# Attention outputs kept transposed: raw rows and softmax sums stored, scaled block by block on GpSimd, loaded as the projection's operand

## The chip, the cores and the metric

One core of a Trainium2 chip runs the whole program. The metric is the device time in microseconds (us) of that core, as a median of several runs. The engines named are TensorE (PE), VectorE (DVE), ScalarE (ACT), GpSimd (POOL) and SyncE (SP), which here only issues transfers.

## The reference

The program computes one transformer layer on 8 x 256 tokens of width 512: cross attention with 32 query heads in 8 key/value groups, then a mixture of experts. What the change touches is the end of the attention:

```python
score = jnp.einsum('bhqd,bhkd->bhqk', qh, kh) / math.sqrt(HEAD_DIM)
attn = jax.nn.softmax(score, axis=-1)
out = jnp.einsum('bhqk,bhkd->bhqd', attn, vh)
out = out.transpose(0, 2, 1, 3).reshape(N, S_, EMBED)
return out @ Wfc.T + bfc
```

Before it the input is normalised and q, k, v are projected. After it come the residual, a second normalisation, a router over 8 experts, a shared expert of double width, and two routed experts for each token.

## The kernel before, in words

Engines run queues of their own, in an order written out by hand, and meet at semaphores. Nothing reorders: an instruction that waits holds up everything behind it on its engine.

**Attention** runs over 16 units: unit u is block u // 4 (512 tokens, 2 of the 8 sequences) and head quarter u % 4 (8 heads). A unit has four groups j of 4 heads and one sequence; G = 4u + j counts them to 64. For each G, PE makes four score fills (line 1303), ACT four exponentials (line 1027), and PE multiplies the probabilities by V in two parts (`pv_part`, line 1317). V carries a column of ones, so that each head's output of 16 rows comes with a 17th, the softmax sum, in strips of 32 partitions of one PSUM bank. Between them PE fills scores for the row maxima of unit u + 2 (line 1231), which DVE reduces (line 1699, four for a pair of groups); at j = 0 PE transposes the maxima of unit u + 1 and DVE negates them (`neg_max_part`, lines 1756 and 1759). After each G, ACT copies the 256 columns of output out of PSUM (`attn_out`, line 1018). After each pair of groups PE transposes the outputs (`pair_transpose`, line 1334), DVE takes the reciprocals of the sums (line 1826) and multiplies (line 1828), and SP stores a unit's rows to `attn_dram` (line 516).

**GpSimd beside it** runs a loop t = 0 to 15. For t < 10 it waits for the maxima of unit t + 2 or so (`nm_done`), cuts half an expert's weights into two 16-bit parts (`cut_weights`: lines 820, 803, 813) and issues the load of the half after next (line 791). For all t it loads a tile of x (line 835), adds the output bias (line 840) and stores the sum as `xb_dram` (line 842). After the loop it loads and cuts the ten held weight halves h (`load_held`, line 794; lines 803 and 813 for even h, while DVE takes odd h at line 1928), and then the shared expert's down weights (lines 860, 864).

**Projection stage**, 16 tiles t of 128 tokens: SP loads a tile's attention rows (line 532) and its `xb` row (line 535). PE transposes the attention rows (line 1395), ACT copies them (line 1037), PE projects (`out_project`, line 1403), DVE adds the residual (`residual_norm`, line 1892) and normalises (line 1902), PE transposes again (line 1412) and computes the router's logits (line 1421). ACT also makes the first part of held half h = t - 2 within tile t (`first_part`, line 1069). SP and ACT both wait for all 16 `xb` stores ahead of the stage. The experts follow (lines 1467 and 1479).

## Time and profile before

| | |
|---|---|
| median of 3 runs | 791.48 us (788.52 to 794.94) |
| the profiled execution's own time | 791.93 us |
| its span | 790.1 us |
| attention, from first to last score and V product | about 103 to 294 us |
| projection stage, to the first product of the experts | about 296 to 383 us |
| experts | about 383 to 790 us |

The span is the time from the program's first to its last instruction in the profile; about 1.8 us lie around it. All times of rows are counted from the span's start.

### The profile page before, as it was taken

Reading aid. Unit: us, or ns where it says so; the run is one execution under the profiler, and the core shown is the slowest. Engines: PE = TensorE matmul, PEld = TensorE weight load, DVE = VectorE, ACT = ScalarE, POOL = GpSimd, SP = SyncE. Lnnn points to the kernel's source line nnn. Section 1 sums busy time; section 2 is a strip of 40 time slices with the busy share of each in tenths; the row PEclk is TensorE's granted clock in tenths of the full one; section 3 lists DMA queues with packets and bytes.
Section 4 is the critical chain, followed back from the end, with each engine's and each line's share of the span. In section 5 each row is a group of like instructions: output and inputs, shape, how many; then the busy total and the mean of one; then the engine's idle time right before and its main releaser. Section 6 shows DMA issues by size and latency. Waiting matters only on the chain.

```text
span 790.1 us, 16078 instructions
## 1 busy us (share of the span) xinstructions
PE 760.1 (96%) x5151; PEld 407.0 (52%) x5152; DVE 579.7 (73%) x1194; ACT 429.3 (54%) x843; POOL 269.3 (34%) x224
## 2 busy tenths in 40 slices
PE   6998999999999989999999999999999999999897
PEld 4553533343433325656755556555555555555553
DVE  4777779999999976998789886555555555547666
ACT  3666579999999973566433553434344343322231
POOL 3263008999993301665300101111111111015331
PEclk9999989999999999999999999999999999999999
DMA  8898846556645798998598576876777777559985
GB/s 330 324 405 245 250 139 211 185 168 194 195 121 172 228 331 295 331 376 275 173 232 225 137 173 137 187 174 175 183 175 180 179 180 173 126 164 288 288 240 150
DMA packets 161782, 172.07 MB, mean 218 GB/s; under 512 B 103680, under 2 KB 117504, under 8 KB 161216
## 3 DMA queue, kind: packets, MB, share of 16 engines
q1 hardware_dynamic: 150012, 128.89, 56.5%
q0 software_dynamic: 11120, 41.43, 16.8%
q10 hardware_dynamic: 596, 1.07, 0.4%
q8 instruction: 30, 0.49, 0.3%
q14 instruction: 24, 0.20, 0.1%
HBM read 105.40 MB, written 42.73 MB: 187 GB/s over the span
## 4 chain that ended last, share of the span: by engine, by line
PE 77%; DVE 10%; DMA 7%; ACT 2%; issue 2%; SPq 1%; DVEq 0%; ACTq 0%
PE psum L1467 29%; PE psum L1479 15%; PE psum L1317 8%; PE psum L1303 6%; PE psum L1231 4%; PE psum L1403 4%; PE psum L1207 4%; PE psum L1334 2%; DMA sb_weights<-in_wdn 2%; DMA sb_weights<-attn_dram 2%; PE psum L1183 1%; DMA sb_hT<-sb_h 1%; DMA sb_weights<-x_dram 1%; DMA sb_weights<-in_ctxT 1%; DVE sb_rows L1902 1%
## 5 line engine op out<-in xcount | busy, mean ns | idle before, releaser
L1467 PE MATMUL psum<-sb_weights,sb_rows 128*128 (+1 forms) x1608 | 250.8, 313 | 0.5 <-DMA sb_rows<-xnT_dram 0.5
L1467 PEld LDWEIGHTS psum<-sb_weights,sb_rows 128*128 128x128 f16 x1608 | 157.2, 98 | 91.8 <-DMA sb_rows<-xnT_dram 1.0
L1027 ACT ACTIVATE sb_weights<-psum,sb_rows 128x512 f32<-128x512 f32 x256 | 158.3, 683 | 16.9 <-PE psum L1303 15.0
L1699 DVE TENSOR_REDUCE sb_rows<-psum 128x4 f32<-128x1024 f32 x128 | 149.9, 1213 | 5.5 <-PE psum L1231 5.5
L1479 PE MATMUL psum<-sb_weights,sb_hT 128*128 (+1 forms) x630 | 147.4, 379 | 2.2 <-DMA sb_hT<-sb_h 2.2
L894 POOL DMA_INDIRECT sb_rows<-xn_rows,sb_slot_tok x39 | 38.2, 980 | 218.1 <-DVE sb_rows L2288 147.9
L1479 PEld LDWEIGHTS psum<-sb_weights,sb_hT 128*128 128x128 f16 x630 | 61.4, 98 | 67.5 <-DMA sb_hT<-sb_h 3.1
L1303 PE MATMUL psum<-sb_weights 50*128 50x512 f16 x256 | 90.0, 391 | 3.0 <-ACT sb_weights L1027 2.6
L1096 ACT ACTIVATE psum<-psum 128x352 f32<-128x352 f32 x71 | 31.8, 448 | 111.8 <-DVE psum L1949 111.8
L1317 PE MATMUL psum<-sb_weights 128*32 128x256 f32 x1024 | 82.9, 396 | 0.0
L1231 PE MATMUL psum<-sb_weights 48*128 48x256 f16 x512 | 73.2, 275 | 0.5 <-DVE sb_rows L1699 0.4
L914 POOL DMA_INDIRECT sb_weights<-slot_y,sb_p_i x32 | 31.4, 982 | 82.7 <-DMA slot_y<-sb_rows 41.7
L1949 DVE SCALAR_TENSOR_TENSOR psum<-psum,sb_inv_now,sb_h 128x352 f32<-128x352 f32 x39 | 23.1, 593 | 49.2 <-PE psum L1467 49.2
L1403 PE MATMUL psum<-sb_weights 128*128 128x512 f32 x128 | 58.5, 600 | 0.0
L1303 PEld LDWEIGHTS psum<-sb_weights 50*128 50x128 f16 x256 | 23.5, 93 | 63.5 <-ACT sb_weights L1027 59.3
L1962 DVE SCALAR_TENSOR_TENSOR sb_h<-psum,sb_h_scale_i,sb_h 128x352 f16<-128x352 f32 x71 | 41.3, 582 | 18.8 <-ACT sb_h L1101 18.6
L1091 ACT ACTIVATE sb_h<-psum,sb_inv_now 128x352 f32<-128x352 f32 x39 | 21.6, 553 | 55.2 <-PE psum L1467 55.2
L1101 ACT ACTIVATE sb_h<-psum,sb_h_scale_i 128x352 f16<-128x352 f32 x71 | 39.3, 553 | 17.2 <-DVE sb_h_scale_i L1954 17.2
L1207 PE MATMUL psum<-sb_weights 128*128 128x512 f16 x192 | 44.9, 380 | 3.7 <-issue 1.9
L803 POOL TENSOR_TENSOR sb_weights<-sb_weights,sb_w_scale_i 128x1408 f32<-128x1408 f32 x15 | 38.5, 2570 | 28.0 <-ACT sb_weights L1069 27.2
L1091 ACT ACTIVATE sb_h<-psum,sb_w_inv_i 128x352 f32<-128x352 f32 x32 | 17.7, 554 | 55.0 <-PE psum L1467 39.2
L813 POOL TENSOR_TENSOR sb_weights<-sb_weights 128x1408 f16<-128x1408 f32 x15 | 42.9, 2861 | 1.2
(264 smaller groups left out, 1017.9 us busy)
## 6 DMA issues: line engine op xcount, KB each, us to landing
sb_weights<-in_wgu SPq DMA_DIRECT2D x20, 704.0 KB, 7.4
sb_weights<-in_wgu POOLq DMA_DIRECT2D x20, 704.0 KB, 5.6
sb_weights<-in_wdn SPq DMA_DIRECT2D x17, 768.0 KB, 5.9
slot_y<-sb_rows SPq DMA_DIRECT2D x39, 256.0 KB, 2.3
sb_weights<-q_parts SPq DMA_DIRECT2D x96, 64.0 KB, 2.2
x_dram<-sb_rows SPq DMA_DIRECT2D x24, 256.0 KB, 4.6
q_parts<-sb_weights SPq DMA_DIRECT2D x16, 256.0 KB, 4.6
sb_rows<-in_x POOLq DMA_DIRECT2D x16, 256.0 KB, 4.8
```

The lines of the kernel that those rows point to most:

```text
L813: nc.gpsimd.tensor_tensor(low, stage, high, ALU.subtract).then_inc(gu_cut, 1)
L1027: nc.scalar.activation(probs[G % 2][:, kt, pair * 512:(pair + 1) * 512], bank[4 + f % 2], ACT.Exp, scale=exp_scale[:, n:n + 1]).then_inc(e ...
L1091: nc.scalar.activation(silu_out[par], two_parts(bank[GU_BANKS[par][0]]), ACT.Silu, scale=inv).then_inc(sil_done, 1)
L1207: mm = nc.tensor.matmul(bank[Q_BANKS[n][m]], wq16[:, wp, k, m * P:(m + 1) * P], xnT[n % 2][:, xp, k, :], start=(k == 0 and i == 0), stop=( ...
L1231: mm = nc.tensor.matmul(bank[banks[qt] + side][:, h * SEQ:(h + 1) * SEQ], q_st[s][lo:hi, g, h, b * SEQ + qt * P:b * SEQ + (qt + 1) * P], k ...
L1303: nc.tensor.matmul(bank[4 + side].rearrange("p (h t) -> p h t", h=HH), k_st[s][lo:hi, g, b * SEQ + kt * P:b * SEQ + (kt + 1) * P], q_st[s] ...
L1317: mm = nc.tensor.matmul(bank[6][VW * c:VW * (c + 1), 0:SEQ], v_now, probs[G % 2][:, kt, c * SEQ:(c + 1) * SEQ], start=(kt == 0), stop=(kt ...
L1403: mm = nc.tensor.matmul(bank[2 + s][:], oT[s][:, k, :], wfc_sb[:, k, :], start=(k == 0), stop=(k == KD - 1))
L1467: mm = nc.tensor.matmul(bank[GU_BANKS[par][which]][:, 0:F], x_T[:, xp * D + k * P:xp * D + (k + 1) * P], gu(wp, k, which), start=(k == 0 a ...
L1479: mm = nc.tensor.matmul(bank[Y_BANKS[par]][:], hT[par][:, hp, j, :], dn(wp, j), start=(j == 0 and n == 0), stop=(j == NF - 1 and n == 2))
L1699: nc.vector.tensor_reduce(to[:, :, j // UB, :, j % UB, qt], psum[:, banks[qt] * 512:(banks[qt] + 2) * 512] .rearrange("p (a h k) -> p a h ...
L1962: nc.vector.scalar_tensor_tensor(h16[par][:, 1, 0:F], bank[GU_BANKS[par][1]][:, 0:F], h_scale[:, par:par + 1], h16[par][:, 0, 0:F], ALU.mu ...
```

## The change

ACT no longer copies after each group but 512 columns after each pair of groups. SP stores a unit's raw transposed rows (`o_parts`, four transfers) and its sums (`o_sums`, one). PE's `pair_transpose` and DVE's normalisation disappear. For each block of four units, GpSimd loads the sums, DVE takes 128 x 128 reciprocals in one instruction (`sum_recs`) at a fixed place in its order (j = 3 of units 5, 9 and 13, and tile 2 of the projection stage for the last block), and GpSimd stores them (`o_recs`). GpSimd then handles each of the 16 units as a chunk i: two loads (rows, and reciprocals repeated over 16 partitions), a multiplication of 128x512, and a store in 512-byte pieces to `attnT_dram`. Chunks 0 to 10 lie in iterations t = 5 to 15 of its loop, chunk 11 behind the loop, chunks 12 to 15 among the held halves. The projection loads its operand in that layout, up to four tiles ahead; the transposes of line 1395 and ACT's copies of line 1037 are gone.

```diff
-    attn_dram = dram("attn_dram", (TILES, P, D))
+    o_parts = dram("o_parts", (BLOCKS, KD, P, BT))
+    o_sums = dram("o_sums", (BLOCKS, KD, MG * HPG, BT))
+    o_recs = dram("o_recs", (BLOCKS, KD, MG * HPG, BT))
+    attnT_dram = dram("attnT_dram", (TILES, P, KD, P))
...
+        chunk_raw, chunk_rec = [words(at, D) for at in chunk_at], [words(at + D, D) for at in chunk_at]
+        def chunk_set(i):
+            return 0 if i < 6 else 1 if i < 3 * KD else 1 + i % 2
...
             def store_attn(u):
-                sp.wait_ge(attn_done, UG * (u + 1))
-                n, m = u // KD, u % KD
-                sp.dma_start(attn_dram[n * TPB:(n + 1) * TPB, :, m * P:(m + 1) * P].rearrange("a p c -> p a c"),
-                             attn_u[u % 2]).then_inc(attn_st[u % 2], 16)
+                sp.wait_ge(pv_evac, MG * (u + 1))
+                n, m, st = u // KD, u % KD, o_st[u % 2]
+                sp.dma_start(o_sums[n, m].rearrange("(g c) t -> c g t", c=HPG),
+                             st[HD:HD + VW * (HPG - 1) + 1:VW]).then_inc(attn_st[u % 2], 16)
+                for c in range(HPG):
+                    sp.dma_start(o_parts[n, m].rearrange("(g c d) t -> c d g t", g=MG, c=HPG)[c],
+                                 st[VW * c:VW * c + HD]).then_inc(attn_st[u % 2], 16)
...
-            def load_attn(b, s):
-                sp.dma_start(a_in[s], attn_dram[bass.ds(b * 2 + s, 1)].rearrange("o p d -> (o p) d")).then_inc(a_ld[s], 16)
+            def load_attn(t):
+                if t >= TPB:
+                    sp.wait_ge(fc_ready, t - TPB + 1)
+                sp.wait_ge(chunk_st, 16 * KD * (t // TPB + 1))
+                sp.dma_start(oT_rows[t % TPB], attnT_dram[t].rearrange("p k t -> p (k t)")).then_inc(a_ld[t % TPB], 16)
...
                 if u == 15:
-                    sp.wait_ge(attn_st[0], FREE + 16 * BATCH)
+                    sp.wait_ge(attn_st[0], FREE + O_ST * UNITS // 2)
                     for s in range(2):
                         sp.wait_ge(xb_st[s], 16 * TILES // 2)
-                    load_res_rows(0, 0)
+                    for s in range(2):
+                        load_res_rows(0, s)
                 store_attn(u)
                 if u == 13:
-                    for s in range(2):
-                        sp.wait_ge(attn_st[s], FREE + 16 * 2)
                     sp.wait_ge(gu_cut, CUTS_P2)
-                    for s in range(2):
-                        load_attn(0, s)
+                    for t in range(TPB):
+                        load_attn(t)
...
+            def load_sums(n):
+                for s in range(2):
+                    pool.wait_ge(attn_st[s], FREE + O_ST * KD // 2 * (n + 1))
+                nc.gpsimd.dma_start(sum_sb, o_sums[n].rearrange("m h (q t) -> (m h q) t", t=P)).then_inc(sum_ld, 16)
+            def store_recs(n):
+                pool.wait_ge(rec_done, n + 1)
+                nc.gpsimd.dma_start(o_recs[n].rearrange("m h (q t) -> (m h q) t", t=P), sum_sb).then_inc(rec_st, 16)
+            def load_chunk(i):
+                n, m, s = i // KD, i % KD, chunk_set(i)
+                pool.wait_ge(rec_st, 16 * (n + 1))
+                if i > 0:
+                    pool.wait_ge(chunk_st, 16 * (i - i % 2 if i >= (BLOCKS - 1) * KD else i))
+                nc.gpsimd.dma_start(chunk_raw[s], o_parts[n, m]).then_inc(chunk_ld, 16)
+                nc.gpsimd.dma_start(chunk_rec[s],
+                                    o_recs[n, m].unsqueeze(1).broadcast_to([MG * HPG, HD, BT])).then_inc(chunk_ld, 16)
+            def scale_chunk(i, loaded):
+                n, m, s = i // KD, i % KD, chunk_set(i)
+                pool.wait_ge(chunk_ld, 32 * loaded)
+                nc.gpsimd.tensor_tensor(chunk_raw[s], chunk_raw[s], chunk_rec[s], ALU.mult).then_inc(chunk_done, 1)
+                pool.wait_ge(chunk_done, CHUNK_SEEN + i + 1)
+                nc.gpsimd.dma_start(attnT_dram[n * TPB:(n + 1) * TPB, :, m, :].rearrange("a p t -> p a t"),
+                                    chunk_raw[s].rearrange("p (a t) -> p a t", a=TPB)).then_inc(chunk_st, 16)
             pool.wait_ge(w_fc, 48)
             load_x(0)
             for t in range(TILES):
                 if t < CUTS_P2:
                     pool.wait_ge(nm_done, t + 3)
+                i = t - TPB - 1
+                if i >= 0:
+                    load_chunk(i)
+                if t % TPB == 0 and t > 0:
+                    load_sums(t // TPB - 1)
+                if t < CUTS_P2:
                     cut_weights(t)
                 if t + 1 < TILES:
                     load_x(t + 1)
                 add_bias(t)
+                if i >= 0:
+                    scale_chunk(i, i + 1)
+                if t % TPB == 0 and t > 0:
+                    store_recs(t // TPB - 1)
+            load_chunk(3 * KD - 1)
+            scale_chunk(3 * KD - 1, 3 * KD)
...
-            pool.wait_ge(attn_done, UNITS * UG)
+            pool.wait_ge(pv_evac, UNITS * MG)
+            load_sums(BLOCKS - 1)
             pool.wait_ge(dn_max_done, NE + SH)
             for h in range(3):
                 load_held(h)
+            store_recs(BLOCKS - 1)
+            last = (BLOCKS - 1) * KD
             for c in range(CUTS_P2, CUTS):
                 h = c - CUTS_P2
+                if h == 0:
+                    for i in range(last, last + 2):
+                        load_chunk(i)
                 if h % 2 == 0:
                     scale_weights(c)
                     second_part(c)
                 else:
                     pool.wait_ge(gu_cut_v, h // 2 + 1)
+                if h == 1:
+                    for i in range(last, last + 2):
+                        scale_chunk(i, last + 2)
+                    for i in range(last + 2, last + 4):
+                        load_chunk(i)
+                if h == 3:
+                    for i in range(last + 2, last + 4):
+                        scale_chunk(i, last + 4)
...
-            def attn_out(G):
-                act.wait_ge(pv_ready, G + 1)
-                if G >= 4:
-                    act.wait_ge(ot_ready, G // 2 - 1)
-                nc.scalar.copy(o_raw[G % 4], bank[6][:, 0:SEQ]).then_inc(pv_evac, 1)
+            def attn_out(p):
+                u, g = p // MG, p % MG
+                act.wait_ge(pv_ready, UB * (p + 1))
+                act.wait_ge(attn_st[u % 2], FREE + O_ST * (u // 2))
+                nc.scalar.copy(o_st[u % 2][:, g, :], bank[6]).then_inc(pv_evac, 1)
...
-                if G > 0:
-                    attn_out(G - 1)
-            attn_out(UNITS * UG - 1)
-            def ot_evac(t, s):
-                act.wait_ge(ota_ready, t + 1)
-                nc.scalar.copy(oT[s], bank[s][:].rearrange("p (k t) -> p k t", k=KD)).then_inc(ota_evac, 1)
+                if G > 0 and G % UB == 0:
+                    attn_out(G // UB - 1)
+            attn_out(UNITS * MG - 1)
...
-                if kt == 0 and G > 0:
-                    pe.wait_ge(pv_evac, G)
+                if kt == 0 and G > 0 and b == 0:
+                    pe.wait_ge(pv_evac, G // UB)
                 v_now = v_res[u // KD][:, b * UB + kt, MG * (u % KD) + g, :]
                 for c in range(HPG):
-                    mm = nc.tensor.matmul(bank[6][VW * c:VW * (c + 1), 0:SEQ], v_now,
+                    mm = nc.tensor.matmul(bank[6][VW * c:VW * (c + 1), b * SEQ:(b + 1) * SEQ], v_now,
...
-            def ot_transpose(t, s, n):
-                pe.wait_ge(a_ld[s], n * 16 + 16)
-                if not (isinstance(t, int) and t < 2):
-                    pe.wait_ge(ota_evac, t - 1)
-                for k in range(KD):
-                    tr = nc.tensor.transpose(bank[s][:, k * P:(k + 1) * P], a_in[s][:, k * P:(k + 1) * P], ident[:])
-                tr.then_inc(ota_ready, 1)
-            def out_project(t, s):
-                pe.wait_ge(ota_evac, t + 1)
+            def out_project(t, r, n):
+                pe.wait_ge(a_ld[r], n * 16 + (16 + A_SEEN))
...
+            def sum_recs(n):
+                dve.wait_ge(sum_ld, 16 * (n + 1))
+                nc.vector.reciprocal(sum_sb, sum_sb).then_inc(rec_done, 1)
...
-                if j % 2 == 1 and G > 2:
-                    normalise(G - 3)
+                if j == UG - 1 and u % KD == 1 and u > 1:
+                    sum_recs(u // KD - 1)
...
+                if t == 2:
+                    sum_recs(BLOCKS - 1)
...```

DVE's order around unit 9, before (the two copies of the normalisation, lines 1826 and 1828, stand at j = 1 and j = 3):

```order
L1756 TENSOR_SCALAR sb_rows<-psum 32x128 [waits nm_in2,mxt_ready]
L1759 SCALAR_TENSOR_TENSOR sb_rows<-psum,sb_rows 32x128 [waits nm_first]
L1699 TENSOR_REDUCE sb_rows<-psum 128x2x2 [waits max_ready] x2
L1826 RECIPROCAL sb_rows<-psum 128x16 [waits ot_ready]
L1828 TENSOR_TENSOR sb_rows<-psum,sb_rows 128x4x64 [waits rec_done]
L1699 TENSOR_REDUCE sb_rows<-psum 128x2x2 [waits max_ready] x4
```

And in the changed kernel (`tile_cmp` holds the block's sums, `sum_ld` counts their loads by GpSimd):

```order
L1765 TENSOR_SCALAR sb_rows<-psum 32x128 [waits nm_in0,mxt_ready]
L1768 SCALAR_TENSOR_TENSOR sb_rows<-psum,sb_rows 32x128 [waits nm_first]
L1708 TENSOR_REDUCE sb_rows<-psum 128x2x2 [waits max_ready] x6
L1831 RECIPROCAL sb_tile_cmp<-sb_tile_cmp 128x128 [waits sum_ld]
L1708 TENSOR_REDUCE sb_rows<-psum 128x2x2 [waits max_ready] x2
```

The normalisation after every pair of groups is gone, and between the maxima of every fourth unit stands one instruction that waits for a transfer that GpSimd issues.

GpSimd's iteration t = 8, before:

```order
L820 TENSOR_TENSOR sb_weights<-sb_weights,sb_w_scale_i 128x1408 [waits gu_ld0,nm_done]
L803 TENSOR_TENSOR sb_weights<-sb_weights,sb_w_scale_i 128x1408 [waits gu_first]
L813 TENSOR_TENSOR sb_weights<-sb_weights 128x1408 [waits gu_scaled]
L835 DMA sb_rows<-in_x 128x512 [waits xb_st1,gu_cut]
L840 TENSOR_TENSOR sb_rows<-sb_rows,sb_weights 128x512 [waits xb_ld0]
L842 DMA xb_dram<-sb_rows 128x512 [waits xb_done]
```

And in the changed kernel:

```order
L853 DMA sb_weights<-o_parts 128x512 [waits chunk_st,rec_st,nm_done]
L854 DMA sb_weights<-o_recs 128x1x512
L842 DMA sb_tile_cmp<-o_sums 128x128 [waits attn_st1,attn_st0]
L815 TENSOR_TENSOR sb_weights<-sb_weights,sb_w_scale_i 128x1408 [waits gu_ld0]
L798 TENSOR_TENSOR sb_weights<-sb_weights,sb_w_scale_i 128x1408 [waits gu_first]
L808 TENSOR_TENSOR sb_weights<-sb_weights 128x1408 [waits gu_scaled]
L830 DMA sb_rows<-in_x 128x512 [waits xb_st1,gu_cut]
L835 TENSOR_TENSOR sb_rows<-sb_rows,sb_weights 128x512 [waits xb_ld0]
L837 DMA xb_dram<-sb_rows 128x512 [waits xb_done]
L860 TENSOR_TENSOR sb_weights<-sb_weights 128x512 [waits chunk_ld]
L862 DMA attnT_dram<-sb_weights 128x4x128 [waits wq_low]
L846 DMA o_recs<-sb_tile_cmp 128x128 [waits rec_done]
```

Chunk 3 and the sums of block 1 have come in: five transfers and a multiplication more, and at its top a wait for the store of the chunk before (`chunk_st`).

## Rows read from the trace of the kernel before

**Rows 1.** Two stretches: length; busy PE, PEld, DVE, ACT, POOL; clock; DMA share; GB/s.
```profile
180.00:210.00 30.00, 30.00 (x312) 11.87 (x316) 28.26 (x37) 27.78 (x52) 28.25 (x18) 1.00 0.59 188
330.00:360.00 30.00, 27.61 (x124) 16.74 (x123) 27.42 (x54) 16.81 (x33) 16.54 (x11) 1.00 1.01 374
```

**Rows 2.** Timeline of ACT, two pairs of groups (start, us, instruction, idle before).
```profile
205.59 2.43 ACT L1027 ACTIVATE sb_weights<-psum,sb_rows 128x512 f32<-128x512 f32 x4 [0.31 <-PE psum L1303]
207.93 0.37 ACT L1018 COPY sb_rows<-psum 128x256 f32<-128x256 f32 x1
208.22 2.49 ACT L1027 ACTIVATE sb_weights<-psum,sb_rows 128x512 f32<-128x512 f32 x4
210.60 0.37 ACT L1018 COPY sb_rows<-psum 128x256 f32<-128x256 f32 x1
211.44 2.43 ACT L1027 ACTIVATE sb_weights<-psum,sb_rows 128x512 f32<-128x512 f32 x4 [0.47 <-PE psum L1303]
```

**Rows 3.** Timeline of PE: the transposes of one pair.
```profile
204.58 0.66 PE L1334 MATMUL psum<-sb_ident,sb_rows 128*128 128x128 f32 x4
```

**Rows 4.** Timeline of GpSimd, from the start of t = 4 to that of t = 7.
```profile
168.68 2.54 POOL L820 TENSOR_TENSOR sb_weights<-sb_weights,sb_w_scale_i 128x1408 f16<-128x1408 f32 x1
...
200.45 0.58 POOL L791 DMA_DIRECT2D sb_weights<-in_wgu  x1 [0.30 <-POOL sb_weights L813]
...
201.58 1.29 POOL L840 TENSOR_TENSOR sb_rows<-sb_rows,sb_weights 128x512 f32<-128x512 f32 x1
203.16 0.56 POOL L842 DMA_DIRECT2D xb_dram<-sb_rows  x1 [0.30 <-POOL sb_rows L840]
203.75 2.55 POOL L820 TENSOR_TENSOR sb_weights<-sb_weights,sb_w_scale_i 128x1408 f16<-128x1408 f32 x1
```

**Rows 5.** GpSimd again: a load that waits for a store; the first held halves.
```profile
237.50 0.56 POOL L842 DMA_DIRECT2D xb_dram<-sb_rows  x1 [0.30 <-POOL sb_rows L840]
240.77 0.54 POOL L835 DMA_DIRECT2D sb_rows<-in_x  x1 [2.70 <-DMA xb_dram<-sb_rows]
...
298.79 1.60 POOL L794 DMA_DIRECT2D sb_weights<-in_wgu  x3 [31.46 <-DVE sb_dn_max L1836]
315.18 2.71 POOL L803 TENSOR_TENSOR sb_weights<-sb_weights,sb_w_scale_i 128x1408 f32<-128x1408 f32 x1 [14.79 <-ACT sb_weights L1069]
...
321.12 0.59 POOL L794 DMA_DIRECT2D sb_weights<-in_wgu  x1 [0.30 <-POOL sb_weights L813]
323.00 0.55 POOL L794 DMA_DIRECT2D sb_weights<-in_wgu  x1 [1.29 <-DVE sb_weights L1928]
...
342.99 0.58 POOL L794 DMA_DIRECT2D sb_weights<-in_wgu  x1 [0.30 <-POOL sb_weights L813]
```

**Rows 6.** DMA issues from 100 to 300 us: KB each, us to landing.
```profile
sb_weights<-q_parts SPq DMA_DIRECT2D x78, 64.0 KB, 2.2
sb_rows<-in_x POOLq DMA_DIRECT2D x16, 256.0 KB, 4.8
xb_dram<-sb_rows POOLq DMA_DIRECT2D x16, 256.0 KB, 3.7
```

**Rows 7.** GpSimd's indirect gathers (line 894): ns min/median/max, start.
```profile
L894 POOL DMA_INDIRECT sb_rows<-xn_rows,sb_slot_tok x39: 940/940/2364, 449.9 to 664.1; - x39
```

**Rows 8.** Timeline of DVE in unit 9, j = 3, and in tile 0.
```profile
222.82 0.26 DVE L1826 RECIPROCAL sb_rows<-psum 128x16 f32<-128x16 f32 x1 [0.18 <-PE psum L1334]
...
302.86 0.69 DVE L1892 TENSOR_TENSOR sb_rows<-psum,sb_rows 128x512 f32<-128x512 f32 x1 [4.66 <-PE psum L1403]
```

**Rows 9.** Groups of DVE by line, 100 to 400 us: busy, mean ns.
```profile
L1826 DVE RECIPROCAL sb_rows<-psum 128x16 f32<-128x16 f32 x32 | 7.9, 247 | 2.9 <-PE psum L1334 2.7
L1656 DVE RECIPROCAL sb_rs_a<-sb_std 128x1 f32<-128x1 f32 x16 | 2.5, 154 | 0.5 <-ACT sb_std L1051 0.5
```

**Rows 10.** Timeline of SP: the first load of an `xb` row.
```profile
294.63 0.33 SPq L535 DMA_DIRECT2D sb_rows<-xb_dram  x1
```

**Rows 11.** Landing of GpSimd's weight loads (line 794), min/median/max.
```profile
DMA to landing us min/median/max: 5.5/7.0/9.8
```

136 lines of the change are left out of this document (44 added, 92 removed).

## The prediction

> **What bounds the kernel now.** I read the busy times by stretch first. In the middle of the attention PE is busy all of 30 us, DVE 28.3, ACT 27.8 and GpSimd 28.3 [rows 1]: four engines are within 8% of full, so taking work from one gains little, and giving work to any costs at once. Then the timeline of ACT: two groups take 211.44 - 205.59 = 5.85 us, with idle times of 0.31 and 0.47 us that end with PE's scores [rows 2]; those come behind the pair's transposes, 0.66 us on PE [rows 3]. So ACT and PE set the pace together, a unit in 11.7 us. Then GpSimd: iterations t = 4 to 6 take (203.75 - 168.68) / 3 = 11.69 us, with no idle time beyond 0.3 us behind its own instructions [rows 4]. GpSimd is already as slow as a unit. In the projection stage (330 to 360 us) DVE is busy 27.4 of 30 us, and the DMA engines all the time [rows 1].
>
> **The change, part by part.** The sum is made against the profiled execution's 791.9 us, 0.4 above the median.
>
> *PE, ACT and DVE in the attention.* The transposes go. Two copies of 0.37 us, each of which holds up the next exponential by 0.29 (207.93 to 208.22) [rows 2], become one of 512 columns, which I put at their sum of 0.58. ACT can give back at most its idle times, 0.3 to 0.5 us of 5.85. I take 5.55 us a pair, 11.1 a unit: 32 x 0.3 = 9.6 us, if nothing else waits. PE's next limit is then ACT itself. DVE loses about 0.7 us a pair. SP issues five stores a unit where it issued one, about 2 us more at 0.4 each in 11.1 us; it stays ahead.
>
> *GpSimd's iterations.* A chunk adds two load issues of 0.56, a multiplication of 128x512 (1.28, as the bias of the same size), 0.3 until it is seen, and a store issue of 0.56 [rows 4]: 1.1 + 2.2 us. At the top it waits for the store before. The row for that wait: a store issued at 237.50 lets the next load start at 240.77, 3.3 us later [rows 5], so 2.7 behind its issue. Iterations 6 and 7 thus take 11.7 + 1.1 + 2.2 + 2.7 = 17.7 us, against a unit's 11.1. For 64 KB of sums or reciprocals I take 2.6 us to landing (2.2 for 64 KB on SP, 3.7 for GpSimd's stores of 256 KB [rows 6]).
>
> Step by step, from the span's start: t = 4 begins at 168.7 as before [rows 4], and adds two issues: t = 5 begins at 181.5. It waits 2.0 for the reciprocals' store: 17.0 us, to 198.5. Iterations 6 and 7: to 233.9. In t = 8 the load of block 1's sums is issued behind chunk 3's loads, at 233.9 + 2.7 + 1.1 = **237.7**, and lands at 240.3.
>
> *DVE's wait.* The instruction that needs it stands where DVE is at 222.82 before (unit 9, j = 3) [rows 8]; at the new pace that is 103 + 119.8 x 5.55 / 5.85 = 216.7. DVE stands still from 216.7 to 240.3. Behind it are the maxima of unit 11; PE gets through about one more group of scores, then ACT starves too. The reciprocals take 1.0 us by the slope between 1 and 16 elements, (247 - 154) / 15 = 6.2 ns each [rows 9], so DVE goes on at 241.3, **18.5 us later than before** at this place. The 9.6 us saved are no part of the sum from here on: GpSimd sets the time.
>
> *The second such wait.* GpSimd: rest of t = 8 (0.6 + 11.1 + 2.2 + 0.6) to 252.2; t = 9, 2.0 + 1.1 + 11.1 + 2.2, to 268.6. From t = 10 no cut hides the loads: 2.7 + 0.6 + 4.8 to landing [rows 6] + 2.2 = 10.3 us each, to 289.2. In t = 12 the sums' load is issued at 293.0, and DVE is released at 296.6. DVE gets there four units after 241.3, at 285.7, and before at 222.8 + 46.8 = 269.6: now 27.0 later. The attention's rest of 24.7 us ends at about 320, not 294.3.
>
> *The start of the projection stage.* SP and ACT want all 16 `xb` stores. The last is issued in t = 15: 289.2 + 10.9 (t = 12) + 9.6 (t = 13) + 10.3 (t = 14) = 320.0, and 5.4 into t = 15, at 325.4. It lands at 329 (3.7 [rows 6]). SP's first `xb` row was asked for at 294.63 [rows 10]; now at 329, landed at 334. DVE's first tile starts at 334, not 302.9 [rows 8]: **+31 us**.
>
> *The held halves.* GpSimd ends t = 15 at 330.3 and chunk 11 at 340.6, and issues the first held load at 341.2 (298.8 before [rows 5]); with 7.0 to landing [rows 11] tile 2 barely waits. Block 3's reciprocals come after tile 2: 315.5 + 31 + 1.0 = 347.6, stored and landed at 350.2. Four chunk loads, 2.2, to 352.4. Half 0 (5.9, as 315.18 to 321.12) to 358.3; before 321.1 [rows 5]: +37. In h = 1: 0.6 + two scalings and stores 4.4 + wait 2.7 + four issues 2.2, so half 4 is asked for at 368.2, before 323.0: +45. h = 2 to 374.7, h = 3 with chunks 14 and 15 to 379.7, h = 4 to 386.2, before 343.0: +43. ACT's first parts sit inside the tiles' order, so the tiles follow these loads. Two or three us come back as later loads are prefetched, and from tile 12 on each tile may gain up to 0.6 (the transposes of line 1395 gone): +40 at the stage's end. The experts are unchanged. The down weights' cuts end about as much later as the stage does, and keep their lead.
>
> **Sum:** 791.9 + 40 = **832 us**.
>
> *Rule against row.* The store row gives 3.3 us until a dependent load can start. The Trainium skill (DMA: Bandwidth & Descriptors, "Anatomy of one DMA") gives a GpSimd transfer about 2.0 us plus its bytes over 436 GB/s, an estimate of 2.6 us for 256 KB. By the rule each of some ten such waits would be 0.7 shorter, and the time about 826 by estimate; the rows go first.
>
> **Bounds.** All new transfers at the fastest rows: stores 2.6 between issue and dependent start, loads 3.0, sums 2.2, weights 5.5 [rows 11]. Some ten waits are then 0.7 shorter, eight loads 1.8, and three weight loads 1.5: about 26 us less in all, 806. Dearer: the trace has no plain GpSimd store in 512-byte pieces and no repeated load. The nearest from above are the indirect gathers at 0.94 us [rows 7]; at 0.38 more for each of some 60 new issues on the path, 22 us, 854; with landings a little slower, 858. I take 0.56, since these transfers are plain.
>
> **The rivals.**
> 1. *Dearer descriptors.* GpSimd's issues cost 0.94 us and more. For: 512 pieces instead of 128, a source with a repeated axis. Against: 704 KB and 256 KB both cost about 0.57 [rows 4]. Result: 854 to 870. The same section of the Trainium skill says that many descriptors can be emitted before their cost shows; that speaks against it, and the issues above bear it out for larger rows only.
> 2. *GpSimd's lag is smaller and partly taken back.* With every chunk wait covered, an iteration is 15.0 us: the sums of block 1 land near 230, and the two stalls are 13 us and little. Then the loads in the tiles weigh less and the prefetch of four tiles shows: 795 to 806.
> 3. *Faster.* DVE never waits, because the sums' load of block 1 has landed before 216.7. It must be issued by 214.1, and the three iterations 5 to 7 would have 214.1 - 181.5 - 3.8 = 28.8 us, 9.6 each. That is the point from which it decides; it is less than the old iteration of 11.69 [rows 4]. In its favour is only that the instructions are few. Then 9.6 us fall away in the attention and up to 10 (16 x 0.66) in the stage: 772 to 784.
> 4. *No change:* GpSimd late, but saved idle time elsewhere pays it back, 784 to 799.
>
> **How the numbers follow.** Forecast with its range 806 to 858: 0.79. Rival 1 above 858: 0.07. Rival 2: 0.07. Rival 3: 0.03. Rival 4: 0.04. The forecast and rival 1 share the mechanism, and rival 2 reaches below 800 with about 0.01. A measurement of this kernel tells about 1% from no change, 8 us: faster 0.03, within 0.05, slower 0.92. The range 806 to 858 leaves out about 0.2.
>
> **What would show it.** In the profile after: DVE idle for about 20 us ahead of the reciprocals of 128x128, released by the load of the sums, near 217 to 240 us, and again about 10 us near 286; PE and ACT idle in the same places, PE's clock perhaps lower behind them. GpSimd without long idle times from 180 to 340, iterations of 17 to 18 us and then 10. Pairs of groups of about 5.55 us before 216. DVE's first residual tile near 334. The first held load near 341. The experts' 407 us unchanged. The prediction is wrong if the load of the sums is issued before 217, if the stall at unit 9 is under 5 us, or if the stage starts before 315 us.

## The result and the profile after

The changed kernel takes **871.31 us** (median of 4 runs, 869.5 to 874.96), the kernel before 792.45 beside it: ratio 1.1006, 95% interval 1.0946 to 1.1066. The forecast was 832, with a range of 806 to 858: the sign and the place were right, the size was half of what came, 40 us for 79. The profiled span is 867.7 us.

The busy times by stretch of the changed kernel (instruction counts in brackets; granted clock, DMA share and GB/s at the end), against [rows 1]:

```profile
180.00:210.00 30.00, 27.34 (x260) 9.13 (x255) 22.24 (x24) 24.26 (x42) 21.41 (x19) 0.86 0.65 189
330.00:360.00 30.00, 16.95 (x67) 5.79 (x63) 10.49 (x9) 5.29 (x10) 11.89 (x15) 0.73 0.70 232
```

Where four engines were full, none is now, and at 330 to 360 us, where the stage ran, the DMA engines have time too. Every engine waits for something that is slow without being busy. GpSimd's timeline, against [rows 4], shows what it is: one iteration from a chunk's loads to the next.

```profile
182.51 0.55 POOL L846 DMA_DIRECT2D o_recs<-sb_tile_cmp  x1
186.34 0.54 POOL L853 DMA_DIRECT2D sb_weights<-o_parts  x1 [3.29 <-DMA o_recs<-sb_tile_cmp]
186.88 0.67 POOL L854 DMA_DIRECT2D sb_weights<-o_recs  x1
187.55 2.56 POOL L815 TENSOR_TENSOR sb_weights<-sb_weights,sb_w_scale_i 128x1408 f16<-128x1408 f32 x1
...
199.26 1.29 POOL L860 TENSOR_TENSOR sb_weights<-sb_weights 128x512 f32<-128x512 f32 x1
200.84 0.83 POOL L862 DMA_DIRECT2D attnT_dram<-sb_weights  x1 [0.29 <-POOL sb_weights L860]
205.49 0.54 POOL L853 DMA_DIRECT2D sb_weights<-o_parts  x1 [3.83 <-DMA attnT_dram<-sb_weights]
206.03 0.64 POOL L854 DMA_DIRECT2D sb_weights<-o_recs  x1
206.67 2.56 POOL L815 TENSOR_TENSOR sb_weights<-sb_weights,sb_w_scale_i 128x1408 f16<-128x1408 f32 x1
```

206.67 - 187.55 = 19.1 us an iteration, 11.7 before. The new work is 0.54 + 0.64 + 1.29 + 0.29 + 0.83 = 3.6 us; the rest is the wait of 3.83 for the store just issued. Over the whole run, by group (busy time, mean ns, then idle time ahead and what ended it):

```profile
L860 POOL TENSOR_TENSOR sb_weights<-sb_weights 128x512 f32<-128x512 f32 x16 | 20.3, 1271 | 20.5 <-DMA sb_weights<-o_recs 20.3
L862 POOL DMA_DIRECT2D attnT_dram<-sb_weights x16 | 13.1, 817 | 4.7 <-POOL sb_weights L860 4.7
L854 POOL DMA_DIRECT2D sb_weights<-o_recs x16 | 10.2, 639 | 1.8 <-issue 1.8
L853 POOL DMA_DIRECT2D sb_weights<-o_parts x16 | 8.8, 548 | 53.7 <-DMA attnT_dram<-sb_weights 38.8 <-DMA o_recs<-sb_tile_cmp 14.9
L1831 DVE RECIPROCAL sb_tile_cmp<-sb_tile_cmp 128x128 f32<-128x128 f32 x4 | 3.8, 952 | 26.7 <-DMA sb_tile_cmp<-o_sums 26.7
L1272 PE MATMUL psum<-sb_weights 48*128 48x256 f16 x512 | 76.8, 291 | 26.4 <-DVE sb_rows L1708 13.3 <-DMA sb_weights<-k_parts 13.0
```

GpSimd works 59 us on the 16 chunks (the first four rows' busy time and their idle times behind its own multiplications and issues). It stands 74.0 us for landings, that is, until a transfer's data have arrived: 20.3 for loads of reciprocals, 38.8 for chunk stores, 14.9 for stores of reciprocals. PE's first projection, at 298.30 before, comes at 337.14, and these are GpSimd's marks behind it, against [rows 5]:

```profile
349.83 0.56 POOL L837 DMA_DIRECT2D xb_dram<-sb_rows  x1 [0.31 <-POOL sb_rows L835]
365.65 1.62 POOL L789 DMA_DIRECT2D sb_weights<-in_wgu  x3
376.01 0.56 POOL L846 DMA_DIRECT2D o_recs<-sb_tile_cmp  x1 [8.73 <-DVE sb_tile_cmp L1831]
389.87 0.58 POOL L789 DMA_DIRECT2D sb_weights<-in_wgu  x1 [0.30 <-POOL sb_weights L808]
422.70 0.61 POOL L789 DMA_DIRECT2D sb_weights<-in_wgu  x1 [0.30 <-POOL sb_weights L808]
```

The first held load is 66.9 us late (298.79 before), and the end of half 4 (the last row: the load that is issued behind it) 422.70 - 342.99 = 79.7 us, which is the whole loss. From there on the kernel is nearly what it was. PE's first product of the experts, before and after:

```profile
382.94 3.74 PE L1467 MATMUL psum<-sb_weights 128*128 128x352 f16 x24
463.69 3.75 PE L1477 MATMUL psum<-sb_weights 128*128 128x352 f16 x24 [1.28 <-DMA sb_weights<-xnT_dram]
```

That is 80.8 us later, and from it to the span's end are 404.0 us for 407.2 before, so the experts add nothing to the loss.

GpSimd had 31.46 us of idle time ahead of the first held load before; the first 12 chunks used it up and added 66.9, 98 us in all, 8.2 each.

### The profile page after: what moved, and what is told of

It reads as the page before. It is cut to its first block, busy times and chain, and to the rows that moved or that the text cites. A ratio compares the mean times of both kernels' runs of the same rounds, so it can differ in the third digit from the quotient of the medians.

```text
span 867.7 us, 15451 instructions
## 1 busy us (share of the span) xinstructions
PE 767.9 (88%) x4959; PEld 394.5 (45%) x4960; DVE 575.8 (66%) x1134; ACT 422.9 (49%) x795; POOL 327.4 (38%) x296
## 4 chain that ended last, share of the span: by engine, by line
PE 50%; POOL 18%; DMA 16%; DVE 7%; issue 6%; ACT 2%; SPq 1%; POOLq 0%; DVEq 0%; ACTq 0%
PE psum L1477 28%; PE psum L1489 15%; DMA attnT_dram<-sb_weights 5%; DMA sb_weights<-o_recs 5%; POOL sb_weights L808 4%; PE psum L1248 3%; POOL sb_weights L798 3%; POOL sb_weights L815 3%; POOL sb_weights L860 2%; DMA o_recs<-sb_tile_cmp 2%; DMA sb_weights<-in_wgu 2%; POOL sb_rows L835 1%; PE psum L1224 1%; POOL sb_weights L853 1%; DMA sb_rows<-xb_dram 1%
## 5 line engine op out<-in xcount | busy, mean ns | idle before, releaser
L1477 PE MATMUL psum<-sb_weights,sb_rows 128*128 (+1 forms) x1608 | 250.8, 313 | 0.0
L1477 PEld LDWEIGHTS psum<-sb_weights,sb_rows 128*128 128x128 f16 x1608 | 157.3, 98 | 91.2 <-DMA sb_rows<-xnT_dram 0.4
L1074 ACT ACTIVATE sb_weights<-psum,sb_rows 128x512 f32<-128x512 f32 x256 | 161.6, 689 | 56.8 <-PE psum L1344 53.8
L1708 DVE TENSOR_REDUCE sb_rows<-psum 128x4 f32<-128x1024 f32 x128 | 153.1, 1216 | 29.7 <-PE psum L1272 28.9
L1344 PE MATMUL psum<-sb_weights 50*128 50x512 f16 x256 | 100.4, 434 | 1.3 <-ACT sb_weights L1074 1.2
L1272 PE MATMUL psum<-sb_weights 48*128 48x256 f16 x512 | 76.8, 291 | 26.4 <-DVE sb_rows L1708 13.3
L1358 PE MATMUL psum<-sb_weights 128*32 128x256 f32 x1024 | 94.6, 447 | 2.4 <-ACT sb_rows L1065 2.4
L1419 PE MATMUL psum<-sb_weights 128*128 128x512 f32 x128 | 65.9, 663 | 0.0
L1272 PEld LDWEIGHTS psum<-sb_weights 48*128 48x128 f16 x512 | 24.9, 98 | 47.8 <-DVE sb_rows L1708 19.5
L808 POOL TENSOR_TENSOR sb_weights<-sb_weights 128x1408 f16<-128x1408 f32 x15 | 43.1, 2873 | 1.2
## 6 DMA issues: line engine op xcount, KB each, us to landing
slot_y<-sb_rows SPq DMA_DIRECT2D x39, 256.0 KB, 2.4
x_dram<-sb_rows SPq DMA_DIRECT2D x24, 256.0 KB, 4.5
q_parts<-sb_weights SPq DMA_DIRECT2D x16, 256.0 KB, 4.1
sb_rows<-in_x POOLq DMA_DIRECT2D x16, 256.0 KB, 5.4
```

Of the source, the lines that this page charges most:

```text
L808: nc.gpsimd.tensor_tensor(low, stage, high, ALU.subtract).then_inc(gu_cut, 1)
L1074: nc.scalar.activation(probs[G % 2][:, kt, pair * 512:(pair + 1) * 512], bank[4 + f % 2], ACT.Exp, scale=exp_scale[:, n:n + 1]).then_inc(e ...
L1272: mm = nc.tensor.matmul(bank[banks[qt] + side][:, h * SEQ:(h + 1) * SEQ], q_st[s][lo:hi, g, h, b * SEQ + qt * P:b * SEQ + (qt + 1) * P], k ...
L1344: nc.tensor.matmul(bank[4 + side].rearrange("p (h t) -> p h t", h=HH), k_st[s][lo:hi, g, b * SEQ + kt * P:b * SEQ + (kt + 1) * P], q_st[s] ...
L1358: mm = nc.tensor.matmul(bank[6][VW * c:VW * (c + 1), b * SEQ:(b + 1) * SEQ], v_now, probs[G % 2][:, kt, c * SEQ:(c + 1) * SEQ], start=(kt ...
L1419: mm = nc.tensor.matmul(bank[2 + r % 2][:], oT[r][:, k, :], wfc_sb[:, k, :], start=(k == 0), stop=(k == KD - 1))
```

## The experiments

"Time" is the median, and ratio and interval are against the kernel before, run beside it. The marks are read from the timelines of one profiled execution each: "projection" is when PE's first projection starts, "held" when the first held load is issued, "half 4" when the load behind half 4 is issued. The last two columns count from these marks to that same execution's own time. A name such as "e9: e2, loads first" means the kernel e2 with one thing more.

| kernel | projection | held | half 4 | time | ratio (95%) | from held | from half 4 |
|---|---|---|---|---|---|---|---|
| before | 298.3 | 298.8 | 343.0 | 792.4 | | 493 | 448.9 |
| e2: no chunks | 292.2 | 300.4 | 342.3 | 790.8 | 1.000 (0.997 to 1.003) | 490 | 447.8 |
| e5: e2, one store | 291.3 | 299.9 | 340.8 | 790.0 | 0.998 (0.994 to 1.002) | 490 | 449.5 |
| e9: e2, loads first | 290.6 | 301.2 | 342.8 | 789.5 | 0.996 (0.992 to 0.999) | 493 | 451.4 |
| e16: blocks 0-2 only | 337.2 | 366.4 | 403.7 | 853.6 | 1.075 (1.069 to 1.082) | 488 | 450.7 |
| e15: last block only | 288.3 | 299.9 | 358.2 | 811.0 | 1.021 (1.014 to 1.027) | 512 | 454.2 |
| changed | 337.1 | 365.7 | 422.7 | 871.3 | 1.101 (1.095 to 1.107) | 504 | 446.8 |
| e1: sums on SP | 317.1 | 367.8 | 421.5 | 872.1 | 1.100 (1.093 to 1.108) | 507 | 453.7 |
| e11: loads first | 340.0 | 368.3 | 426.0 | 874.4 | 1.105 (1.098 to 1.111) | 506 | 448.4 |
| e13: e1 and e11 | 312.9 | 370.3 | 423.8 | 869.1 | 1.094 (1.087 to 1.101) | 502 | 448.2 |
| e7: no multiplication | 329.9 | 354.4 | 409.9 | 859.8 | 1.089 (1.085 to 1.094) | 504 | 448.8 |
| e4: two buffers | 324.5 | 345.4 | 404.3 | 854.7 | 1.080 (1.072 to 1.088) | 507 | 448.6 |
| e8: e4 + e1, loads ahead | 325.4 | 340.7 | 400.0 | 848.3 | 1.071 (1.063 to 1.079) | 510 | 450.9 |
| e14: e8, loads first | 309.4 | 332.9 | 393.6 | 843.9 | 1.063 (1.057 to 1.069) | 514 | 453.4 |
| e6: by tile, in place | 303.9 | 319.8 | 362.4 | 819.9 | 1.038 (1.033 to 1.042) | 505 | 462.7 |
| e12: e6, loads first | 298.8 | 315.7 | 359.4 | 821.0 | 1.035 (1.029 to 1.042) | 507 | 463.6 |
| e17: e13 in another order | 310.4 | 331.8 | 432.9 | 888.1 | 1.126 (1.119 to 1.133) | 550 | 449.2 |

**Is it GpSimd's chain at all?** e2 drops the sums, reciprocals and chunks and projects the raw rows (it leaves out the normalisation):

```diff
-                if i >= 0:
-                    load_chunk(i)
...
-                if i >= 0:
-                    scale_chunk(i, i + 1)
```

> Leaves out the normalisation: GpSimd's sums, reciprocals and chunks are gone, and so is DVE's 128x128 reciprocal; the projection loads the raw transposed rows straight from o_parts, in 512-byte pieces. PE, ACT, DVE and SP keep the change otherwise, with SP's five stores a unit. Theory G (GpSimd's serial chain of transfers and waits sets the time): everything lost comes back and what the removed transposes and copies are worth shows: 778 to 792 us, projection stage starting near 295 us. Rival S (SP's queue is full with five stores a unit, so the loads of the next units come late and PE's clock falls in the gaps): units of 12 to 15 us remain without any chunk, and the time stays above 805 us.

Nothing is left of the loss. Nor is there a gain from what the change takes off PE, ACT and DVE; more on that below.

**Is it the waits of DVE and PE in the attention?** e1 has SP issue the sums' loads of blocks 0 to 2 as soon as the unit's stores have landed.

> The changed kernel with one thing moved: the loads of the sums of blocks 0 to 2 are issued by SP at the start of units 5, 9 and 13, not by GpSimd behind its chunks, so that DVE no longer waits for GpSimd's place in its order. Theory G: DVE's 26.7 us of waits go and the attention ends some 15 to 25 us earlier, but GpSimd reaches its last xb store and its held halves no earlier, and the projection stage waits for these: 866 to 873 us, no change. Rival W (the two long DVE waits, with the half clock behind them, are what costs): 840 to 850 us.

DVE's waits for the sums fell from 26.7 to 6.2 us, the projection came 20 us earlier, and the time did not move. e11 issues SP's twelve loads of unit u + 3 ahead of the maxima's rows, e13 does both:

```diff
             for u in range(1, UNITS - 3):
-                nm_rows(u + 1)
                 sp.wait_ge(pv_ready, u * UG)
                 load_unit((u + 3) // KD, (u + 3) % KD)
+                nm_rows(u + 1)
```

> The changed kernel with the same exchange. Theory R: the ring is what the chunks' landings lengthen in the attention (k_parts waits 28.5 us in 16, units of 12.2 to 16.3 us), so the loads issued 2 to 3 us earlier take 15 to 28 us off: 843 to 856 us. Theory G alone (GpSimd's chain sets the attention's pace, since its sums' reciprocals hold DVE and its stores come late): within 5 us of 871.

> The changed kernel with both: the sums of blocks 0 to 2 loaded on SP's queue, and SP's twelve loads of a unit ahead of the maxima's rows. If the two waits of the attention (DVE for the sums, TensorE for k_parts) cover each other, both at once give what neither gave alone, at least 8 us: 850 to 864 us, with the first projection at 325 us or earlier. If GpSimd's own chain (its last store of x plus bias, its held loads behind chunk 11) sets the stage's start, the attention ends earlier and the time does not follow: 867 to 875 us.

My guess for e11 was wrong: the waits for `k_parts` went, those for the sums grew from 26.7 to 33.4 us. With both away the attention does end 24 us sooner, and the stretch behind it in e13 is this:

```profile
330.00:360.00 30.00, 0.00 (x0) 0.00 (x0) 0.00 (x0) 0.00 (x0) 13.93 (x17) 0.50 0.50 146
```

PE, DVE and ACT do nothing for 30 us. GpSimd's chain, on its own path, is where it was:

```profile
351.09 0.57 POOL L849 DMA_DIRECT2D xb_dram<-sb_rows  x1 [0.30 <-POOL sb_rows L847]
...
370.28 1.62 POOL L801 DMA_DIRECT2D sb_weights<-in_wgu  x3
```

These rows decide it: **in the changed kernel the attention's stalls, which look worst in the profile, cost nothing; they lie beside GpSimd's chain.**

**How the loss divides.** e15 keeps the chain for the last block alone, e16 for the first three (each projects the other blocks without normalisation).

> The chain for the last block alone: blocks 0 to 2 are projected from the raw rows without normalisation, block 3 goes through sums, reciprocals and chunks 12 to 15 as in the changed kernel. This is the stage's share. From the trace of the changed kernel: its h0 half ends 24.2 us after the first held load was issued, which is 19.4 us after the same point of the kernel before, and the two round trips of the four chunks keep two more halves 5.6 us and more behind: 812 to 832 us. If the last block's chain lies beside the held halves for the most part (rival: the stage's loss is the late start alone), under 805 us.

> The chain for blocks 0 to 2 alone: block 3 is projected from the raw rows. This is the attention's share and what GpSimd still owes when it ends (chunks 9 to 11 and four bias tiles at 337 to 365 us): the loss of 79 us less what the last block alone loses if the two add up, 835 to 850 us. If the two overlap, it stays over 855 us.

16 us by the ratio for the last block, 60 for the others: 76 of 79, they add up. So do the ends of half 4, which come 15.2 and 60.7 us late, 75.9 of 79.7. The table's last columns say the same: from the first held load to the end it is 502 to 514 us with chunks 12 to 15 in the stage and 488 to 493 without them, but from half 4 it is 447 to 454 us in either case. So the time is the moment when GpSimd is through with half 4, plus a constant. e6 and e12 are the exceptions, and have a limit of their own (below).

**What in a chunk costs?** e7 leaves out only the multiplication. e4 has two buffers, so that a load need not wait for the store just issued. e8 adds e1 and loads each chunk an iteration ahead:

```diff
-            return 0 if i < 6 else 1 if i < 3 * KD else 1 + i % 2
+            return (3 if i % 2 else 0) if i < 5 else 1 if i == 5 else i % 2 if i < 3 * KD else 1 + i % 2
...
+                    if i % KD < KD - 1:
+                        load_chunk(i + 1)
                     scale_chunk(i, i + 1)
```

> The changed kernel, and only the multiplication of each chunk left out (loads, waits and stores stay). Theory G: it takes away 16 times 1.26 + 0.29 us from a chain in series, 25 us, less where another wait ends last: 846 to 856 us, so that 55 us or more of the 79 remain with issues and landings. Rival A (arithmetic and port): the DVE recovers too, under 825 us.

> The changed kernel with two chunk buffers in turn for chunks 0 to 11, so that a chunk's loads no longer wait for the store of the chunk before (10 such waits, 38.8 us, in the changed kernel; 7 of them in chunks 1 to 11). Theory G: the first residual tile comes 20 to 27 us earlier, 845 to 853 us. Rival C (the DMA engines are busy, so that the time goes into later loads in place of the stores): under 8 us gained, 863 us or more.

> The changed kernel with two chunk buffers, each chunk of blocks 0 to 2 loaded an iteration ahead (but the first of a block), and the sums' loads of these blocks on SP's queue. Theory G: the waits for o_parts and o_recs before L860's multiplication (20.3 us in 8) and those for attnT's store (38.8 us in 10) go but for the last block's, leaving 3.3 us of issues and multiplication an iteration and the last block's two round trips: 805 to 828 us. Rival Q (the landings lengthen with what is in flight, the issues themselves are the price): 840 us or more.

All three gave less than I expected. Their groups, first of e7, then of e8:

```profile
L860 POOL DMA_DIRECT2D attnT_dram<-sb_weights x16 | 12.3, 773 | 23.5 <-DMA sb_weights<-o_recs 23.3 <-issue 0.2
L853 POOL DMA_DIRECT2D sb_weights<-o_parts x16 | 8.8, 548 | 66.6 <-DMA attnT_dram<-sb_weights 51.2 <-DMA o_recs<-sb_tile_cmp 15.4
```

```profile
L879 POOL TENSOR_TENSOR sb_weights<-sb_weights 128x512 f32<-128x512 f32 x16 | 20.6, 1286 | 3.7 <-DMA sb_weights<-o_recs 3.6
L872 POOL DMA_DIRECT2D sb_weights<-o_parts x16 | 8.7, 544 | 33.5 <-issue 15.4 <-DMA o_recs<-sb_tile_cmp 9.9 <-DMA attnT_dram<-sb_weights 8.2
```

e7 takes 16 x (1.27 + 0.29) = 25 us of work away and 12 us come back as longer waits for stores (51.2 for 38.8) and 3 for reciprocals (23.3 for 20.3): the multiplication had covered part of a landing. In e8 the waits that end with a landing come down from 74 to 21.7 us in these two rows; 15.4 more (longest 7.97) have no releaser that the trace names. That is worth 23 us of time. What remains is 3.6 us of GpSimd's own time a chunk, the reciprocals' round trip at each block's start, and the last block. And one wait is new: at 299.25 GpSimd has stood 9.68 us for DVE's reciprocals of block 2. With GpSimd ahead, the attention's pace is no longer free; In e14 below, whose attention is faster, that wait is gone and the first held load comes 7.8 us sooner.

**Without the round trip.** In e6 SP loads a tile's raw rows into the projection's operand and its reciprocals beside it, and GpSimd multiplies in place, 16 times; e12 adds the loads-first order and own buffers for the first four tiles' reciprocals.

```diff
+            def scale_tile(t):
+                a, n = t % TPB, t // TPB
+                pool.wait_ge(a_ld[a], n * 16 + (16 + A_SEEN))
+                pool.wait_ge(rec_ld[t % 2], 16 * (t // 2 + 1))
+                nc.gpsimd.tensor_tensor(oT_rows[a], oT_rows[a], rec_tile(t), ALU.mult).then_inc(tile_done, 1)
```

> The same arithmetic without the round trip: the sums are loaded on SP's queue, the reciprocals stored by tile, the raw rows of a tile loaded straight into the projection's operand with its reciprocals beside it, and GpSimd multiplies them in place (16 times about 1.28 us: four before the stage, two ahead of the held halves, one behind each of the ten). Theory G (the price of the change is GpSimd standing in series with landings): 790 to 806 us, as GpSimd has over 5 us idle in each 10.9 us of two halves, and the multiplications cost at most what DVE loses beside them (10 times up to 1.3 us). Rival A (the price is the arithmetic itself and the port it shares with DVE in the stage): 815 us or more.

> The kernel that multiplies tile by tile in place (819.9 us), with the same exchange on SP's queue and buffers of their own for the first four tiles' reciprocals, so that they are multiplied before the stage (three of the four waited for one buffer: 25.0 us). Theory R and G together: the attention ends some 8 to 12 us earlier and the stage's first projections no longer wait: 796 to 810 us, still not under the kernel before, because the multiplications beside the held halves and the last block's reciprocals stay. If the stage is set by DVE beside GpSimd's multiplications instead (rival A), it stays within 5 us of 815.

This takes back 51 of the 79 us and is the best version of the change, but still 3.8% behind the kernel before and above the 806 and 810 us that I allowed. The number falls to rival A, its mechanism does not: in e6 DVE is busy only 19.55 of 30 us at 360 to 390. DVE instructions beside GpSimd's do take longer (one of the five second parts 4.28 us for 1.67), but the five sum to 12.0 us for 8.4 before, and the normalisation takes 1.28 us on average for 1.40. GpSimd waits for reciprocals that have one buffer (even tiles, and all from 10 on):

```profile
L886 POOL TENSOR_TENSOR sb_weights<-sb_weights,sb_dn_tail 128x512 f32<-128x512 f32 x11 | 17.1, 1555 | 40.4 <-DMA sb_dn_tail<-o_recs 40.2
```

In e12 the projection comes 5 us sooner, and the time stays. Two of its waits between 296 and 410 us (total us, times, longest) name what the stage waits for, SP's and then DVE's:

```profile
SPq L565 <- POOL sb_weights L883: 30.0, 8, 6.5
DVE sb_rows L1917 <- DMA sb_rows<-xb_dram: 12.4, 6, 5.7
```

SP may load the next reciprocals into the one buffer only when GpSimd has multiplied, and while it stands there the `xb` rows behind it in its order are not loaded. It is again a chain of landings, now through SP. e6 has both waits too (29.8 and 10.8 us), and these two kernels need 463 us behind half 4 where the others need 450. That a second buffer would give these 13 us back was not tried.

**Only the order.** e17 is e13 with the last bias tiles ahead of chunk 5 and the held loads ahead of chunk 7.

> The kernel with the sums on SP's queue and the exchanged loads (869.1 us), the same work with GpSimd's order changed from t = 10 on: the bias tiles 10 to 15 first and without chunks, then the reciprocals of block 2, chunks 5 and 6, the three first held loads as soon as the attention has ended, chunks 7 to 9 while those land, 10 and 11 behind half 0, and block 3's two pairs two halves later. Theory H (the time follows the last store of x plus bias and the first held load): both come before 325 us instead of 354 and 370, and the kernel takes 825 to 850 us, over 811 because block 3's chunks stay in the stage and seven others join them. Rival L (the length of GpSimd's chain as a whole sets it, wherever it is served): 860 us or more.

Theory H fell. Both gates came earlier (312.2 and 331.8 for 351.1 and 370.3), and the median is 19 us above e13's, the profiled execution 10 us. SP's waits (total us, times, longest):

```profile
SPq L558 <- DMA attnT_dram<-sb_weights: 83.3, 3, 38.6
```

SP now stands for chunks 7, 11 and 15 with the stage's own stores and loads behind it. Chunks 5 to 11 cost 7 to 15 us each, 11 on average, wherever they lie, and half 4 ends at 432.9, 9 us behind e13's 423.8, though the first held load came 38 us sooner. From there it is 449 us, as elsewhere. The sum of the series up to half 4 counts, not the place of one gate in it. Whether SP's waits alone would have held the stage as long, this run does not tell.

**Why the other half gives nothing.** Copying once a pair, put alone on the kernel before (e3, the copy's bank as in the change, into two buffers in turn):

> The kernel before with one part of the change alone: ACT copies 512 columns after each pair of groups, all else (PE's transposes, DVE's normalisation, the rows stored) as before. ACT saves one fixed part of a copy a pair, at most 0.1 us of 5.85, and the idle times that end with PE's scores stay because the transposes stay: 789 to 792 us, no change. A rival that ACT's copies as such hold up the exponentials: 5 us or more gained.

798.2 us, ratio 1.007 (1.003 to 1.011): slower by 0.7%. ACT of e3, against [rows 2]:

```profile
207.98 2.43 ACT L1027 ACTIVATE sb_weights<-psum,sb_rows 128x512 f32<-128x512 f32 x4 [0.72 <-PE psum L1303]
210.32 0.58 ACT L1018 COPY sb_rows<-psum 128x512 f32<-128x512 f32 x1
210.80 2.51 ACT L1027 ACTIVATE sb_weights<-psum,sb_rows 128x512 f32<-128x512 f32 x4
214.02 2.43 ACT L1027 ACTIVATE sb_weights<-psum,sb_rows 128x512 f32<-128x512 f32 x4 [0.71 <-PE psum L1303]
```

214.02 - 207.98 = 6.04 us a pair for 5.85. The copy itself is 0.58, as I took it, but it now comes as one block of which PE waits 0.20 us at line 1317 and ACT 0.7 behind. With the transposes gone as well (e2) a pair that waits for nothing takes 5.51 us (forecast 5.55), but many do wait for `k_parts`, and the attention ends 6 us sooner, at 292.2. Three more runs ask who eats that:

> The kernel without the normalisation (790.8 us, ratio 0.9999), and each unit's five stores on SP's queue made one store of the same 256 KB (all 128 partitions, the first half of the columns: what is stored is not what the projection needs). Theory S: the shorter pairs of the changed attention are lost because SP spends 0.57 us and four times about 2 us a unit on the five issues, and q_parts, k_parts and the maxima's rows are issued behind them; then TensorE's waits for k_parts (L1248: 8.8 us and 12.1 us of weight loads before) fall under 3 us, a unit takes about 11.1 us, and the kernel takes 778 to 786 us. Rival C: it is the one bank that is copied once a pair (as in the kernel before with the single copy alone, 798.2 us), so that nothing changes: 788 to 793 us, with the waits for k_parts gone and others in their place.

> The kernel without the normalisation (790.8 us), and in SP's loop over the units the twelve loads of unit u+3 issued ahead of the maxima's rows of unit u+1 instead of behind them. Theory R (a ring: negated maxima on DVE, then SP's 1.1 us for the rows and 5.6 us for twelve loads, 2 to 3 us of landing, then TensorE's scores for the next maxima and DVE's reductions of them, again the maxima; 11.7 us fitted it before, the shorter pair does not): TensorE's waits for k_parts (8.8 and 12.1 us) fall under 3 us, a unit comes down from 12.3 to about 11.3 us, and the kernel takes 775 to 785 us. Rival C (the one bank that is copied once a pair): the waits go and others take their place, 788 to 793 us.

> The kernel before with the same two parts of SP's loop exchanged and nothing else. Its units take 11.70 us with TensorE without a wait for k_parts, so the ring does not bind it: 789 to 794 us by both theories; faster by more than 1% would say that the ring held the kernel before too, and then part of the change's possible gain had nothing to do with the change.

e5: the five stores are innocent; they stand behind the loads, where SP waits for the next maxima anyway. e9: PE's waits for `k_parts` vanish and the projection comes 1.7 us sooner. e10: 792.4 us, ratio 0.999 (0.995 to 1.003), so the kernel before had no such wait. In e9 the attention is 8 us shorter than before, and the held loads start 2 us *later*. DVE's rows of e9 say why:

```profile
287.52 5.49 DVE L1812 TENSOR_REDUCE sb_dn_max<-sb_weights 128x1 f32<-128x1536 f32 x3 [4.48 <-DMA sb_weights<-in_wdn]
295.66 1.75 DVE L1812 TENSOR_REDUCE sb_dn_max<-sb_weights 128x1 f32<-128x1536 f32 x1 [2.64 <-DMA sb_weights<-in_wdn]
298.85 1.75 DVE L1812 TENSOR_REDUCE sb_dn_max<-sb_weights 128x1 f32<-128x1536 f32 x1 [1.44 <-DMA sb_weights<-in_wdn]
```

The last maximum of the down weights ends at 300.6, and the held loads wait for it, in [rows 5] too. DVE waits 13.0 us for these weights in e9 (4.8 before). The shorter attention is given back there, to a load. And the stage behind runs at DVE's pace, 28.70 busy of 30 at 330 to 360 us in e2, 27.42 before.

e14 closes the list:

> The kernel with two chunk buffers, chunks loaded an iteration ahead and the sums on SP's queue (848.3 us, first projection at 325.4), with SP's loads exchanged as well. Its attention still waited 14.8 and 16.8 us for k_parts, and GpSimd's chain is out of its way: if that ring is what is left of the attention's loss, the first projection comes at 300 to 310 us and the kernel takes 825 to 838 us. If the landings themselves (two chunks in flight beside the attention's own loads) hold it, the waits move to the maxima's rows and it stays over 843 us.

Waits for `k_parts` gone, projection at 309, but held at 333: 843.9, and 453 us from half 4, as elsewhere.

## Why the prediction was half right

By its own steps:

| step | forecast | measured |
|---|---|---|
| t = 5 begins | 181.5 | 183.06 |
| block 1's sums asked for | 237.7 | 242.57 |
| DVE goes on behind them | 241.3 | 247.28 |
| block 2's sums asked for | 293.0 | 304.89 |
| last `xb` store issued | 325.4 | 349.83 |
| first held load | 341.2 | 365.65 |
| half 0 ends | 358.3 | 389.87 |
| half 4 ends | 386.2 | 422.70 |

- *Mechanism: right.* GpSimd sets the time, through the last `xb` store, the held loads and block 3's chunks. e2, e16 and e15 show it, e13 most of all.
- *The step that failed: the price of a landing on GpSimd's chain*, taken once from one row and then as constants: 2.7 us behind a chunk's store, 2.0 behind the reciprocals', and, where no cut hides them, 5.4 from a chunk's first load issue to its multiplication. Measured: ten waits for chunk stores of 38.8 us, 3.9 on average, up to 6.18; 3.29, 2.91, 3.61 and 5.08 for the reciprocals' stores; 4.8 to 8.9 for the loads.
- *Where it adds up:* the error is 4.9 us when block 1's sums are asked for and 6.5 at the first load of t = 10 (277.76 for 271.3). It grows to 24.5 at the first held load. Of these 18.0, the stores' landings make 9.3 (24.8 for 15.5), the loads' 7.7 (45.5 for 37.8), GpSimd's own work the rest. The loads of `o_parts` follow each other at 289.57, 303.74, 315.56, 333.03, 346.36 and 357.49, 13.6 us on average where I took 10.3. The last block adds 12 more: 10.4 us for 6.4 until its reciprocals are there, 5.6 for 2.6 until they are stored, 32.8 for 27.9 from half 0 to half 4. The 2 or 3 us that I let come back behind half 4 had not come by the experts' start.
- *The issues:* 0.82 and 0.64 us for 0.56, 16 x 0.34 = 5.4 us. Rival 1 had the time nearly right (854 to 870) with a mechanism that gives a fifteenth of the loss.
- *DVE's two stalls:* 13.19 and 11.83 us, forecast 24 and 11. They were there, but as e1 and e13 show they are no term of the sum. I built the start of the stage on them only up to the point where `xb` took over, and that was right.
- *"SP stays ahead": wrong, but it cost nothing.* In the changed kernel PE waits for `k_parts`. SP's loads hang on DVE's maxima, those on PE's scores, those on the loads: a ring that 11.7 us a unit fitted and the shorter unit does not. e11 took the wait away and gained nothing.
- *9.6 us in the attention:* e2 got 6 of them and lost them to the down weights. The sum left them out for another reason, that GpSimd sets the time.
- *The upper bound* of 858 let landings be "a little slower". The rows to ask were the slowest landings, 9.8 us beside a median of 7.0 in [rows 11]: a chain of some 20 waits for landings in series next to other transfers draws from that tail again and again, and in a busy stretch the tail is the rule.

Why the landings were so long can only be read from rows beside each other; no run isolates it. The wait for a store goes roughly with how busy the DMA engines are during it:

| kernel, stores | waits, us (mean DMA share during each) |
|---|---|
| before, `xb`, from 238 us | 2.70 (0.33), 2.98 (0.65), 2.08 (0.36), 3.41 (0.73), 2.06 (0.42) |
| changed, chunks, all ten | 3.83 (0.61), 2.82 (0.52), 2.52 (0.35), 2.83 (0.59), 3.19 (0.28), 5.34 (0.76), 6.18 (1.00), 2.50 (0.35), 4.01 (0.93), 5.57 (0.60) |
| e13, chunks, from 275 us | 8.03 (0.96), 7.73 (0.95), 4.25 (0.54), 2.51 (0.35), 2.50 (0.36), 4.10 (0.79) |
| e17, `xb`, from 275 us | 6.73 (0.88), 2.04 (0.37), 7.36 (0.97), 6.53 (1.02) |

The 2.70 that I took stands in a quiet stretch. The chain grew into the one from about 275 to 340 us, where SP loads the down weights, 768 KB each. In e17, where plain `xb` stores fall into it, they wait as long as the stores in 512-byte pieces, so the pieces alone are not what makes landings long.

## What to carry to other kernels

Work moved "to the engine that has time" is priced by its round trips, not by its arithmetic: here 1.3 us of multiplication came with two loads and a store in series, 8.2 us a chunk. A landing is priced from rows of the stretch in which it will be waited for, not from a quiet one. Before believing the stall that looks largest, ask which engine has an independent path to the end, and take the stall away: if the end does not move, it was cover. And a shorter stage pays only up to the next load that was timed to its old length.

## What the runs showed of the chip

- A store of 256 KB in 512-byte pieces occupies GpSimd's queue for 0.82 us, and a load with a repeated source 0.64, against 0.54 for a plain one.
- From the end of such an issue to the start of a dependent instruction it took 2.50 us at best (DMA share 0.35), and 8.03 in e13 (DMA share 0.96), just after SP had issued three loads of 768 KB at 274.35. The Trainium skill (DMA: Bandwidth & Descriptors, "Anatomy of one DMA") gives about 2.0 us plus the bytes over 436 GB/s, by estimate 2.6 us for 256 KB: that is near this kernel's best case, not its mean of 3.9, and the measurement decides.
- DVE's cut of 128x1408 (line 1930) took 1.67 us in four of its five executions and 4.27 in the one at 419.62, which ran beside GpSimd's cut (2.92 us from 419.49).
- A kernel that stalls also runs at a lower granted clock: 0.86 and 0.73 in the two stretches above, 1.00 in [rows 1]. In e13 it is 0.50, the lower of the two levels, in the stretch where PE does nothing. The eight matmuls of a V product take 1.08 us behind such pauses and 0.64 otherwise, which lengthens the attention's tail. In e13 the attention ends 24 us sooner at the same time, so that too was covered.
